# A row of routing weights sent through DRAM instead of through TensorE

## What is computed

```python
x = x + gnn(layernorm(x), adj)          # convolution branch, message passing, GRU
h = layernorm(x)
weights = (h @ wr + br)[..., 0]          # one routing weight per node
_, idx = top_k(weights, 512)
sel = h[idx[:511]]                       # the 511 best nodes
y = (gelu(sel @ w1 + b1) @ w2 + b2) * weights[idx[:511]]
x = x + h;  x[idx[:511]] += y
```

## Time and profile before

| | |
|---|---|
| median of three runs | 635.34 us (634.87 to 636.11) |
| the profiled execution | 633.39 us, span 631.5 us |
| TensorE (matmul) busy | 92% of the span |
| VectorE busy | 67% |
| ScalarE busy | 54% |
| GpSimd busy | 45% |
| mean granted TensorE clock | 0.97 of full speed |

### The profile page before, as it was taken

One profiled execution on the slowest core, in us unless ns is written; L12 is line 12 of the kernel. 1 busy time (PEld: TensorE's weight loads), 2 busy tenths in 40 slices (PEclk: granted clock), 3 DMA queues, 4 the chain that ended last, 5 costly groups with the idle time before them and its releaser, 6 DMA issues.

```text
span 631.5 us, 8193 instructions
## 1 busy us (share of the span) xinstructions
PE 580.4 (92%) x2656; PEld 424.8 (67%) x2656; DVE 420.9 (67%) x990; ACT 341.3 (54%) x598; POOL 286.9 (45%) x338
## 2 busy tenths in 40 slices
PE   3979999999999999999999999999999997787880
PEld 2766788678867886688668866886688665454450
DVE  6735365678686869686968695869588776329220
ACT  4734467546754665466556654666464634354240
POOL 2710055306552565256534743474335431754763
PEclk9989999999999999999999999999999998879985
DMA  6270600270027002700171016100520151210210
GB/s 221 108 243 2 266 1 0 68 267 1 2 75 280 13 1 61 274 33 2 41 267 60 1 34 224 77 0 23 214 98 1 34 180 56 68 51 26 85 44 29
DMA packets 34073, 55.72 MB, mean 88 GB/s; under 512 B 2274, under 2 KB 23541, under 8 KB 33776
## 3 DMA queue, kind: packets, MB, share of 16 engines
q1 hardware_dynamic: 29936, 48.88, 22.0%
q0 software_dynamic: 4096, 6.33, 2.9%
HBM read 44.68 MB, written 14.75 MB: 94 GB/s over the span
## 4 chain that ended last, share of the span: by engine, by line
PE 83%; issue 6%; POOL 4%; DVE 2%; ACT 2%; DMA 1%; POOLq 0%; DVEq 0%
PE N L1225 16%; PE C L1106 10%; PE C L1107 10%; PE C L1108 10%; PE M L1205 9%; PE D L1201 4%; PE N L1318 2%; PE M L1107 2%; PE M L1108 2%; PE M L1106 2%; PE D L1106 2%; PE D L1107 2%; PE D L1108 2%; POOL sel L485 1%; PE D L1115 1%
## 5 line engine op out<-in xcount | busy, mean ns | idle before, releaser
L648 ACT ACTIVATE tr<-D 128x512 f32<-128x512 f32 x128 | 76.4, 597 | 110.4 <-PE D L1201 103.7
L1201 PE MATMUL D<-V,U 128*128 128x512 f32 x128 | 89.1, 696 | 3.5 <-issue 3.5
L1205 PEld LDWEIGHTS M<-cst,adjb 128*128 128x128 f32 x512 | 63.3, 141 | 40.7 <-issue 20.5
L442 POOL TENSOR_TENSOR ga<-xT,gn 128x512 f32<-128x512 f32 x16 | 20.7, 1292 | 146.3 <-ACT gn L690 146.3
L935 DVE TENSOR_TENSOR tz<-tr,M 128x512 f32<-128x512 f32 x64 | 43.6, 684 | 56.6 <-ACT tr L648 53.1
L1205 PE MATMUL M<-cst,adjb 128*128 128x128 f32 x512 | 77.7, 274 | 1.9 <-DVE ga L935 1.9
L485 POOL DMA_INDIRECT sel<-R,ridx x64 | 63.9, 998 | 24.8 <-issue 17.4
L1225 PE MATMUL N<-tz,msgF 128*128 128x512 f32 x128 | 64.2, 594 | 0.0
L1225 PE MATMUL N<-ga,msgF 128*128 128x512 f32 x128 | 64.2, 593 | 0.0
L935 DVE TENSOR_TENSOR ga<-tr,M 128x512 f32<-128x512 f32 x64 | 43.7, 682 | 21.8 <-ACT tr L648 21.6
L1106 PE MATMUL C<-ef,wc 128*128 128x512 f32 x136 | 56.5, 416 | 0.0
(11 more groups left out here) (223 smaller groups left out, 1478.7 us busy)
## 6 DMA issues: line engine op xcount, KB each, us to landing
adjb<-in_adj SPq DMA_DIRECT2D x8, 4096.0 KB, 13.8
adjb<-sel SPq DMA_DIRECT2D x8, 516.0 KB, 6.4
out<-R SPq DMA_DIRECT2D x8, 512.0 KB, 3.4
xall<-in_x SPq DMA_DIRECT2D x7, 512.0 KB, 5.7
adjb<-in_conv_w SPq DMA_DIRECT2D x1, 1088.0 KB, 8.2
adjb<-in_weights SPq DMA_DIRECT2D x1, 1024.0 KB, 6.1
sel<-R,ridx POOLq DMA_INDIRECT x64, 2.4
xall<-in_x SPq DMA_DIRECT2D x2, 256.0 KB, 3.2
```

Source lines behind the costliest of these rows:

```text
L648: nc.scalar.activation(E[:, u % NE, :], Db[u % NH][:, :], ACT.Exp, scale=-1.0).then_inc(exp_ok, 1)
L1201: MM(Db[h][:, :], U[:, t * P:(t + 1) * P], V[:, half(h)], start=True, stop=True).then_inc(d_ps, 1)
L1205: i = TR(Mb[h][:, k * P:(k + 1) * P], adjb[:, h * TH + k, t * P:(t + 1) * P], ident)
```

## The change

The row of weights no longer goes through TensorE and ScalarE. SyncE waits for `w_ok`, stores the column of 1024 weights to a DRAM tensor `wrow[b]` in node order, waits until that has landed, and loads the 4 KB back into all 128 partitions of W. VectorE's rank step 0 waits for that load (`W_in`) instead of for ScalarE's copies. The 8 transposes and 2 copies of each of the 8 batches go. In SyncE's list the new pair stands ahead of the store of the base rows of the same batch, and for batch 7 behind the first seven `load_sel`. The second half of the GRU, which waited for `W_ok`, now waits for `y2_ok` (VectorE has read the convolution banks).

```diff
+        wrow = [nc.dram_tensor(f"wrow{b}", (N,), F32).ap() for b in range(B)]
...
+            def row_of_weights(b):
+
+                sp.wait_ge(w_ok, b + 1)
+                with nc.allow_non_contiguous_dma("node weights"):
+                    sp.dma_start(wrow[b].rearrange("(t p) -> p t", p=P), R[:, b % 2, :, R_W]).then_inc(wrow_out, 16)
+                sp.wait_ge(wrow_out, 16 * (b + 1))
+                sp.dma_start(W[:, :], wrow[b].unsqueeze(0).broadcast_to([P, N])).then_inc(W_in, 16)
...
                 if b > 0:
+                    row_of_weights(b - 1)
                     store_base(b - 1)
...
                 load_sel(b)
+            row_of_weights(B - 1)
             store_base(B - 1)
...
-            def row_of_weights(b, h, bank_):
-
-                wait(act, wt_ps, b, NH, h + 1)
-                nc.scalar.activation(W[:, half(h)], bank_[:, :], ACT.Copy).then_inc(W_ok, 1)
...
-                    w0 = row_at(b) + 1
-                    if b > 0 and u in (w0, w0 + 1):
-                        row_of_weights(b - 1, u - w0, Cb[u - w0])
...
                 if t == 0:
-                    wait(dve, W_ok, b, NH, NH)
+                    wait(dve, W_in, b, 16, 16)
...
-            def row_of_weights(b, q, h, bank_):
-
-                wait(pe, w_ok, b, 1, 1)
-                for k in range(TH):
-                    w = R[:, q, h * TH + k, R_W:R_W + 1]
-                    i = TR(bank_[:, k * P:(k + 1) * P], w.broadcast_to([P, P]), ident)
-                i.then_inc(wt_ps, 1)
...
-                    if b > 0 and u == row_at(b) + 1:
-                        wait(pe, y2_ok, b, 2, 2)
-                        for h in range(NH):
-                            row_of_weights(b - 1, 1 - q, h, Cb[h])
...
-                else:
-                    wait(pe, W_ok, b - 1, NH, NH)
+                if h == 1:
+                    wait(pe, y2_ok, b, 2, 2)
...
-                    if b == 1 and j == 3:
-                        pe.wait_ge(x1_ok, NH * B)
-                        row_of_weights(B - 1, 1, 0, M1)
-                    if b == 2 and j == 0:
-                        pe.wait_ge(W_ok, NH * (B - 1) + 1)
-                        row_of_weights(B - 1, 1, 1, M1)
```

More of the change, by code:

```diff
@@ L265, in build @@
             sem("xn2_ok"), sem("base_ok"), sem("row_id"), sem("prod_ok"), sem("dot_ok"), sem("w_ok"))
-        wt_ps, W_ok, rank_ok, sum_ok, ridx_ok = (sem("wt_ps"), sem("W_ok"), sem("rank_ok"),
-                                                 sem("sum_ok"), sem("ridx_ok"))
+        wrow_out, W_in, rank_ok, sum_ok, ridx_ok = (sem("wrow_out"), sem("W_in"), sem("rank_ok"),
+                                                    sem("sum_ok"), sem("ridx_ok"))
         sel_out = [sem("sel_out0"), sem("sel_out1")]
@@ L297, in tile @@
             return slice(h * HALF + k * P, h * HALF + (k + 1) * P)
-        def row_at(b):
-            return W_AT if b < B - 1 else W_LAST
         def half(h):
@@ L754, in ffn_step @@
                         normalise2(B - 1, 1, tuple(range(T)))
-                    if b == 2 and j == 0:
-                        row_of_weights(B - 1, 0, M1)
-                    if b == 2 and j == 1:
-                        row_of_weights(B - 1, 1, M1)
             over_batches(act, ffn_step)
```

## The result

The change makes the kernel slower. The kernel after takes 671.0 us (median of four runs, 669.3 to 678.5), beside 635.7 us for the kernel before (its three executions and one more, of 637.7 us); the ratio is 1.0565, with an interval of 1.052 to 1.061: 33 to 39 us, against a forecast of -4.7. The profiled execution took 671.27 us with a span of 669.4 us, 37.9 us over that of before. That profile of before is of a short execution (633.4 us), so differences to it come out some 2 to 4 us larger than those between medians.

The account below looks back on a forecast made before the run. TensorE was taken as the bound, its transposes on the chain. Batches 1 to 6 -5.2, batch 7 -0.3, feed-forward +0.9 gave -4.6, with roundings -4.7 us: 635.3 to 630.6 us, range 627.8 to 638.0.

Parts of the forecast that it names:

- What bounds the kernel: Batches 1 to 7: TensorE sets the pace and its eight transposes lie on the chain, 0.87 us per batch.
- no gain on TensorE: Rival, batches 1 to 7: loop bound by distances, exponential and product, transposes in a gap; 636.2 us, chance 0.06.
- The store: Column of 1024 single weights to DRAM: taken as 3.6 us, like the base-row store with as many pieces; low end 2.0.
- twice: Rival: each small store piece costs double, store 5.0 to 5.4 us; total 633.5 to 634.3 us, chance 0.17.
- The load: One 4 KB row from DRAM into 128 partitions of W: taken as 3.8 us, between 2.8 and 4.04.
- The allowances: Time from weights to VectorE's first read of W, less TensorE's gain: 9.2 us batch 1, 8.7 batches 2-6, 7.0 batch 7.
- L: Time from weights ready to the row in W, by store, load and two reactions: 7.6 us, between 5.0 and 9.6.
- All this costs nothing. GpSimd's scatters are not moved.: SyncE's queue: transfers behind the new pair come later, their consumers have slack, scatters unmoved; priced at no cost.
- the function: Whole kernel, change by L: -7.0 us up to 5.9, -4.7 at 7.6, zero at 10.0, steeper past 11.1.
- late: Rival: W comes over 10 us after the weights; decides from L = 10.0, 637.5 us at L = 11; chance 0.14.

Follow-up runs that it names:

- e5: Kernel after, but weights stored as 128 pieces of 32 bytes, W left in arrival order, rule for equal weights left out: 630.6 us against 637.1 before, ratio 0.989.
- e2: Kernel before plus an unused store of the 1024 weights to DRAM, each word 512 bytes apart: ratio 1.0005 to before.
- e7: Kernel before plus an unused store of the 1024 weights to DRAM, words 64 bytes apart: 0.3% slower than before.
- e11: Kernel before plus an unused store of the 1024 weights to DRAM, words 32 bytes apart: 0.3% slower than before.
- e12: Kernel before plus an unused store of the 1024 weights to DRAM, words 16 bytes apart: 0.4% slower than before.
- e1: Kernel before plus the store of 1024 adjacent single words to DRAM, awaited only by SyncE, result unused: 654.5 us against 637.9, ratio 1.026.
- e10: Kernel before plus an unused store of only 512 of the weights, adjacent in 2 KB of DRAM: ratio 1.020 to before.
- e3: Kernel before plus an unused store of the 1024 single words to a spare SBUF tile instead of DRAM: ratio 0.999 to before.
- e9: e5 plus four further 32-byte-piece stores in series ahead of the row's load, so W comes late: 643.2 us against 637.0 before, ratio 1.0084.

## Why the prediction was wrong, point by point

**What bounds the kernel.** Right. The units shown are 1.53 us apart, and with a quick store (e5) each of batches 1 to 6 takes 0.84 to 0.87 us less and batch 7 1.2 us less. The rival "no gain on TensorE" is refuted.

**The store: the step that failed.** The sum put 3.6 us for it, "it has as many pieces, and I count on no gain from their being small". It took 8.5 us in batch 1, and 10.5 to 11.6 us beside scatters. The nearest row was near in the count of pieces and not in the one thing that counts here: how many separate writes fall into one small stretch of DRAM. Each 512-byte piece of the base store has a stretch of its own; of the single words 16 share 64 bytes. e2, e7, e11, e12 and e1 show the step from 2.6 to 8.9 us with only the spacing changed, e10 that the number of words is not it, e3 that SBUF is not. The high end of 5.0 to 5.4 us came from the rival "twice", and it was a price per piece too. The reading behind it was off as well: isolated words of 4 bytes landed sooner than 512-byte pieces (2.6 us against 3.2 to 3.6). The prediction cites the Trainium skill, page "DMA: Bandwidth & Descriptors", "Specifications", where transfers under 512 bytes are said to be read, modified and written; to DRAM, standing alone, such words took at most 0.6 us more than to SBUF (e2, e7, e3), so next to none of the loss comes from that alone. That it bites when many such writes fall on one place would fit the curve; no run shows what the memory does inside.

**The load.** 4.2 to 5.5 us against 3.8; a term too small by 0.4 to 1.7 us, most in batch 1, where the adjacency load was issued 1.5 us behind it.

**The allowances.** Right in kind, and too small in batches 1 to 6. With the measured L (14.2; 15.6, 16.1, 15.8, 15.6, 15.5; 16.2; 16.0 us) the prediction's own terms give: batch 1 -0.9 + 2.6 = +1.7; batches 2 to 6 +3.6, +4.1, +3.8, +3.6 and +3.5; batch 7 -0.9 + 9.2 = +8.3; the feed-forward +9.3; in all +38. (The forecast's own terms add up to -4.6; it says -4.7.) The spans differ by 37.9 us, the medians by 35.3. That the sum fits so well is luck, since its parts do not. From the weights of one batch to those of the next, by VectorE's timelines, the kernel after loses 0.3, 2.4, 2.7, 3.8, 3.7 and 2.1 us in the stretches that hold the waits of batches 1 to 6, 9.1 us in that of batch 7, and 13.7 us from batch 7's own weights to the end. So batches 1, 2, 3 and 6 lost 1.2 to 1.4 us less each than priced, and the end 4.4 us more. The slack was more than the 2.40 us of idle time that I counted: in e9 nothing is lost up to L = 12.5 in batch 4 and 13.1 in batch 6, where the loss should begin at 11.1.

**A term that the sum does not have: TensorE's clock.** I priced a wait at its length and not at what TensorE's clock does behind it. These are stretches from one batch's weights to the next (length, busy times, granted clock, DMA share, GB/s), batch 4 and the end, first in the kernel before, then after:

```profile
312.26:376.26 64.00, 63.63 (x307) 47.49 (x306) 49.38 (x113) 38.48 (x69) 31.99 (x39) 1.00 0.26 91
561.50:631.50 70.00, 46.78 (x170) 28.38 (x168) 24.58 (x84) 22.06 (x37) 37.97 (x40) 0.85 0.15 46
```

```profile
317.70:385.50 67.80, 64.87 (x299) 47.56 (x298) 50.09 (x113) 36.94 (x67) 31.34 (x39) 0.97 0.37 94
585.70:669.40 83.70, 46.95 (x161) 27.74 (x159) 24.57 (x84) 21.08 (x35) 37.95 (x40) 0.81 0.21 51
```

Batches 4 and 5 are the only ones of 1 to 6 in which the granted clock falls (to 0.97, the others have 1.00), and the only ones that lost 1.1 to 1.6 us more than their neighbours 3 and 6. A mean of 0.97 over 67.8 us is some 4 us at the lower level, which can cost 2 us (an estimate from these rows). At the end 0.81 in place of 0.85 is some 11 us more at the lower level, up to 5 or 6 us if TensorE were the bound all the time; it is not, so this is an upper limit. In e9 the clock of batch 7's stretch is 0.82, where it was 0.89 before, and that of the end 0.83.

**"All this costs nothing. GpSimd's scatters are not moved."** Wrong. They were not moved, but held up: five times the DMA time for the same packets, and the store itself takes 2 to 3 us longer beside them. I asked for each transfer how late it would be, and not what a transfer that does not complete does to the others. e1 prices this alone at 17 us, the clock's part in it included. In the kernel after both costs are there, and they overlap, since an engine that waits for W loses nothing by a stall under it; how much of the 35 us is which was not separated, and the 17 us of e1 cannot be added to the function's 38.

**The rival "late"** was the right one, with a chance of 0.14. Its point of decision, L = 10.0, lies between e5 (6.0, faster) and e9 (11.2 to 13.1, slower). The chance was too small, because "1024 pieces in 1.8 us there" counted as evidence against it, and there is no row at all of single words to DRAM.

**What stays open.** What the writes to one stretch do to each other, and over how large a stretch. What "remote" is. And the 4.4 us at the end beyond the function. About half may be the profile of before, short at that place: from batch 7's own weights to the end e2, e3, e7, e11 and e12, none of which loses more than 0.4%, take 2.3 to 2.6 us more than it. The clock is another part. The chain of the kernel after also holds two pieces there, some 20 and 50 us after the last of these stores has landed:

```profile
619.60 7.33 another core or an unknown queue
...
646.61 5.76 another core or an unknown queue
```

They need no crowded store: the chain of e3 has such a piece of 6.31 us, and in e5, which is faster than the kernel before, an instruction of ScalarE waits 8.05 us and one of VectorE 8.66 us in this way in the feed-forward.

## What to carry to other kernels

Before a column of single words is sent to DRAM, ask how many separate writes fall close together (up to four to 64 bytes cost little here, sixteen cost 6 us): the nearest row must be alike in that, not in the count of pieces or bytes. Make the pieces contiguous first: one transpose on TensorE (0.11 us) or a copy into an adjacent tile brought the store from 8.5 us to 1.2 or 1.4 us and turned a loss of 5.6% into a gain of about 1%. And price a new transfer twice, once for the engine that waits for it and once for the traffic that runs beside it; adding it to the old kernel with nobody waiting (e1) measures the second by itself. Where a wait leaves TensorE idle, look at the granted clock behind it before taking the wait's length for its price. And check a sum by its parts: here one was right in all by two errors that cancel.

## What the runs showed of the hardware

- Stores of single 4-byte words to DRAM, 1024 of them, in batch 1: 2.6 us 64 bytes apart, 2.8 us at 32, 3.3 us at 16, 8.5 to 8.9 us adjacent; half as many adjacent words also 8.7 us. In the kernel after the DMA engines showed about half a us of work for them.
- 4 KB in 128 pieces of 32 bytes landed in 1.4 us, in 8 pieces of 512 bytes in 1.2 us (shortest cases).
- While such a crowded store is unfinished, the packets of GpSimd's scatters take five times as much DMA time (50.1% against 10.1% of 15 us), and exponentials stand waiting for up to 6.9 us (e10) for no cause that the profile shows; with words 16 bytes or more apart it was up to 3.7 us.
- Behind such a wait, with TensorE busy for 4.05 of 7.00 us, its granted clock was 0.50 for the next 3 us.
- A load of one 4 KB row of DRAM into 128 partitions took 4.2 to 5.5 us in the kernel after.
- VectorE's compare-and-count over f32 in SBUF took 1.65 times as long when it read every eighth word (1333 ns against 808).
